# Cross attention with a routed expert layer: six of eight score units as 16-bit pairs, and a new order of norm, dispatch, positions and first period

## What is computed

```python
xn = layernorm(x)
q = xn @ Wq.T + bq;  k = ctx @ Wk.T + bk;  v = ctx @ Wv.T + bv      # 16 heads of 16, 77 context rows
scores = q . k / 4, masked;  attn = softmax(scores)
x = x + (attn . v) @ Wo.T + bo
xf = layernorm(x)
probs = softmax(xf @ w_router);  gate, eidx = top_k(probs, 2);  gate /= sum(gate)
# place of a token in its expert: a running count over all tokens; capacity 768 rows of each of 8 experts
h = relu(expert_in @ w1 + b1);  y = h @ w2 + b2
x = x + sum over the two experts of gate * y
```

## Time and profile before

| | us |
|---|---|
| median of 3 runs | 554.68 (549.78 to 555.1) |
| the profiled execution, its own time | 555.85 |
| its span in the profile | 554.1 |
| TensorE busy | 474.3 (86% of the span) |
| TensorE weight loads busy | 444.1 (80%) |
| VectorE busy | 284.8 (51%) |
| ScalarE busy | 268.3 (48%) |
| GpSimd busy | 234.0 (42%) |
| mean granted TensorE clock | 0.897 |

### The profile page before, as it was taken

One profiled execution on the slowest core, in us unless ns is written; L12 is line 12 of the kernel. 1 busy time (PEld: TensorE's weight loads), 2 busy tenths in 40 slices (PEclk: granted clock), 3 DMA queues, 4 the chain that ended last, 5 costly groups with the idle time before them and its releaser, 6 DMA issues.

```text
span 554.1 us, 10225 instructions
## 1 busy us (share of the span) xinstructions
PE 474.3 (86%) x3757; PEld 444.1 (80%) x3757; DVE 284.8 (51%) x579; ACT 268.3 (48%) x507; POOL 234.0 (42%) x364
## 2 busy tenths in 40 slices
PE   5474989999898978515999999999999999999990
PEld 4353878787777857415999999999999999999990
DVE  3447274788775633211564563745537455465430
ACT  2225254466363541202866765567755577654520
POOL 4612021434744337473043643636436365363531
PEclk9879598999996865655999999999999999999995
DMA  8838289843273101213033341433414334131110
GB/s 259 199 109 265 78 229 279 218 115 123 88 210 115 49 30 48 68 67 117 1 122 101 129 133 39 159 116 141 130 29 165 114 113 147 27 97 38 48 38 1
DMA packets 51767, 63.07 MB, mean 114 GB/s; under 512 B 7515, under 2 KB 46474, under 8 KB 51598
## 3 DMA queue, kind: packets, MB, share of 16 engines
q1 hardware_dynamic: 36118, 41.10, 25.5%
q0 software_dynamic: 6144, 12.64, 6.9%
q10 hardware_dynamic: 9464, 8.79, 5.8%
HBM read 40.97 MB, written 25.72 MB: 120 GB/s over the span
## 4 chain that ended last, share of the span: by engine, by line
PE 59%; POOL 7%; issue 4%; DVE 3%; ACT 1%; DMA 1%; POOLq 0%; DVEq 0%; SPq 0%
PE ps L1161 16%; PE ps L1159 16%; PE ps L1160 16%; POOL expert_in L526 3%; PE ps L1441 2%; PE ps L1260 2%; PE ps L1285 1%; PE ps L1174 1%; PE ps L1304 1%; ACT rows L687 1%; POOL rstd L420 1%; POOL rows L515 1%; DMA xc<-expert_in 1%; DMA expert_in<-rows,sidx 0%; PE ps L1242 0%
## 5 line engine op out<-in xcount | busy, mean ns | idle before, releaser
L792 ACT ACTIVATE hf<-ps,bcol 128x256 f32<-128x256 f32 x192 | 80.0, 468 | 97.1 <-PE ps L1161 97.0
L1159 PE MATMUL ps<-wh,hh 128*128 128x256 f32 x384 | 109.5, 285 | 0.0
L1159 PE MATMUL ps<-xTh,wh 128*128 128x256 f32 x384 | 108.7, 283 | 0.0
L1161 PE MATMUL ps<-xTh,wl 128*128 128x256 f32 x384 | 108.6, 283 | 0.0
L1160 PE MATMUL ps<-xTl,wh 128*128 128x256 f32 x384 | 108.5, 282 | 0.0
L1161 PE MATMUL ps<-wh,hl 128*128 128x256 f32 x384 | 107.7, 280 | 0.0
L1160 PE MATMUL ps<-wl,hh 128*128 128x256 f32 x384 | 107.7, 280 | 0.0
L1110 DVE TENSOR_TENSOR hl<-hf,hh 128x512 fp32r<-128x512 f32 x96 | 66.6, 694 | 78.1 <-ACT hh L798 73.8
L575 POOL DMA_INDIRECT out<-yb,ctok x48 | 51.9, 1082 | 92.8 <-DVE yb L1125 84.3
L567 POOL DMA_INDIRECT acc<-out,ctok x48 | 69.3, 1444 | 37.4 <-issue 22.9
L1159 PEld LDWEIGHTS ps<-xTh,wh 128*128 128x128 f32 x384 | 73.9, 193 | 0.0
(11 more groups left out here) (163 smaller groups left out, 854.7 us busy)
## 6 DMA issues: line engine op xcount, KB each, us to landing
wraw<-in_L_ffn_w SPq DMA_DIRECT2D x16, 1024.0 KB
expert_in<-zrow ACTq DMA_DIRECT2D x6, 1032.0 KB, 7.6
xc<-expert_in SPq DMA_DIRECT2D x24, 258.0 KB
qs<-q_by_head SPq DMA_DIRECT2D x8, 768.0 KB, 5.9
q_by_head<-qh SPq DMA_DIRECT2D x16, 256.0 KB, 2.7
q_by_head<-ql SPq DMA_DIRECT2D x8, 256.0 KB, 3.8
out<-xs SPq DMA_DIRECT2D x4, 512.0 KB
xs<-in_x ACTq DMA_DIRECT2D x1, 1536.0 KB, 11.7
```

The lines of the kernel that those rows point to most:

```text
L792: ins = a.activation(hf[:, i % 2, s * CH:(s + 1) * CH], ps[:, i, s * CH:(s + 1) * CH], ACT.Relu, bias=bcol[:, bass.ds(at(e * MT + 2 * i + ...
L1159: T.matmul(dst, sh, mh, start=first, stop=False)
L1161: return T.matmul(dst, sl, mh, start=False, stop=last)
```

## The change

It has four parts.

1. Of a period's eight units six are split (0, 1, 2, 4, 5, 6) and two plain (3, 7); before it was four and four. `rest_p(i, j)` runs for j = 0 to 5.
2. On POOL a period now reads `tag_rows(n-1)` (the two copies of token number and gate, taken out of `dispatch`), `norm2(n)`, `picks(n-1)`, `dispatch(n-1)`, `norm1(i+3)`, `running(n)`.
3. `positions(n-1)` stands behind `times_v(w,0)` on TensorE, `slot_values(n-1)` and `picked(n-1)` in the first half of VectorE's period. `scores(m,0)` waits for one slot value more from m = 4 on.
4. In the head, q(0) is turned and projected ahead of k. V's projection, Wo's turn, the front of macro tile 2 and the copies and rests of v are in period 0.

VectorE's order within a period is written anew with this; in it `rest_q(f)` comes ahead of `maximum(i+1,0)`, where it came behind it.

```diff
-    NS = NG // 2
+    SPLIT = (0, 1, 2, 4, 5, 6)
+    PLAIN = (3, 7)
+    NS, NF = len(SPLIT), len(PLAIN)
...
@@ POOL
+            def tag_rows(n):
+
+                pool.wait_ge(S["gates_ready"], n + 1)
+                if n >= 2:
+                    pool.wait_ge(S["scattered%d" % (n % 2)], n // 2 * (2 * G * 16))
+                g.tensor_copy(rows[:, n % 2, :, :, TOK], tokid[:, toks(n), :])
+                g.tensor_copy(rows[:, n % 2, :, :, GATE], gt[:, n % 2])
...
+                if n >= 1:
+                    tag_rows(n - 1)
                 if n >= 0:
                     norm2(n)
-                if i + 3 < NM:
-                    norm1(i + 3)
-                if n >= 0 and i < NM:
-                    running(n)
                 if n >= 1:
                     picks(n - 1)
...
                 if n >= 1:
                     dispatch(n - 1)
-                if n >= 0 and i >= NM:
+                if i + 3 < NM:
+                    norm1(i + 3)
+                if n >= 0:
                     running(n)
...
@@ VectorE, the period
-                units, nxt, front, tail, slots = i < NM, i + 1 < NM, 3 <= f < NM, 0 <= w < NM, n >= 0
+                units, nxt, front, tail, slots = i < NM, i + 1 < NM, f < NM, 0 <= w < NM, n >= 0
...
                 if units:
                     rest_p(i, 0)
+                if i == 0:
+                    values()
                 if tail:
                     sum_o(w, 0)
-                if nxt:
-                    maximum(i + 1, 0)
+                if n >= 1:
+                    slot_values(n - 1)
+                if units:
+                    rest_p(i, 1)
                 if front:
                     rest_q(f)
                 if nxt:
-                    maximum(i + 1, 1)
+                    maximum(i + 1, 0)
                 if tail:
                     divide_o(w, 0)
+                if n >= 1:
+                    picked(n - 1)
+                if nxt:
+                    maximum(i + 1, 1)
                 if units:
-                    rest_p(i, 1)
+                    rest_p(i, 2)
                 if i == 0:
-                    v_rest(1)
-                if slots and i >= NM:
-                    picked(n - 1)
+                    v_rest(0)
                 if nxt:
                     maximum(i + 1, 2)
                 if tail:
                     sum_o(w, 1)
+                if units:
+                    rest_p(i, 3)
                 if nxt:
                     maximum(i + 1, 3)
                     split_max(i + 1)
                 if tail:
                     divide_o(w, 1)
-                if units:
-                    rest_p(i, 2)
+                if i == 0:
+                    v_rest(1)
                 if i + 3 < NM:
                     stats1(i + 3)
                 if units:
-                    rest_p(i, 3)
+                    rest_p(i, 4)
+                    rest_p(i, 5)
                 if i == 0:
                     rest_bo()
...
@@ TensorE
-                    if m >= 5:
-                        pe.wait_ge(S["slot_ready"], m - 4)
+                        pe.wait_ge(S["slot_ready"], m - 3)
...
+            turn_xn(0)
+            pe.wait_ge(S["wq_copied"], 1)
+            project_q(0)
             pe.wait_ge(S["wk_copied"], 1)
...
                 if tail:
                     times_v(w, 0)
+                if n >= 1:
+                    positions(n - 1)
```

More of the change, by code:

```diff
@@ L178, in xattn_moe_kernel @@
         pf = at_("pf", [KV, 2, 2 * GT])
[L179 removed]
+        pn = at_("pn", [KV, 2, NF, 2 * GT])
         st = at_("st", [P, G, 6])
@@ L984, in v_rest, with values @@
                 ins.then_inc(S["vpart_step"], 1)
+            def values():
+                dve.wait_ge(S["v_projected"], 1)
+                dve.wait_ge(S["bv_loaded"], 16)
+                dve.wait_ge(S["const_ready"], 3)
+                for b in range(NB):
+                    ins = v.scalar_tensor_tensor(out=vf[:, b * D:(b + 1) * D], in0=bv_b[:], scalar=bscale[0:KV],
+                                                 in1=ps[0:KV, 4, b * D:(b + 1) * D], op0=ALU.mult, op1=ALU.add)
+                ins.then_inc(S["vf_ready"], 1)
             stats1(0)
@@ L989, in _ @@
             normal1(0)
+            stats1(1)
+            dve.wait_ge(S["mask_loaded"], 16)
+            v.tensor_scalar(mb[:, :, 0:NK], mraw[:], 0.0, NEG, ALU.is_equal, ALU.mult).then_inc(S["mask_step"], 1)
+            rest_q(0)
+            normal1(1)
             dve.wait_ge(S["k_projected"], 1)
@@ L1014, in _ @@
             maximum(0, 1, ST)
-            dve.wait_ge(S["v_projected"], 1)
-            dve.wait_ge(S["bv_loaded"], 16)
-            dve.wait_ge(S["const_ready"], 3)
-            for b in range(NB):
-                ins = v.scalar_tensor_tensor(out=vf[:, b * D:(b + 1) * D], in0=bv_b[:], scalar=bscale[0:KV],
-                                             in1=ps[0:KV, 4, b * D:(b + 1) * D], op0=ALU.mult, op1=ALU.add)
-            ins.then_inc(S["vf_ready"], 1)
             maximum(0, 2, SC)
@@ L1090, in _ @@
                     route(n)
-                    if n >= 1 and i < NM:
-                        slot_values(n - 1)
-                if slots:
-                    if n >= 1 and i < NM:
-                        picked(n - 1)
                     gates(n)
@@ L1341, in _ @@
             ins.then_inc(S["k_projected"], 1)
-            turn_xn(0)
-            pe.wait_ge(S["wq_copied"], 1)
-            project_q(0)
             pe.wait_ge(S["wv_loaded"], 16)
@@ L1353, in _ @@
             project_q(1)
-            turn_xn(2)
             pe.wait_ge(S["kst_loaded"], 16 * 4)
             pe.wait_ge(S["mask_copied"], 1)
-            scores(0, 0, SC, 2)
-            scores(0, 1, ST, 2)
-            pe.wait_ge(S["bias_copied"], 1)
-            pe.wait_ge(S["wv_copied"], 1)
-            for b in range(NB):
-                for k in range(KT):
-                    ins = T.matmul(ps[0:KV, 4, b * D:(b + 1) * D], cT[:, k, b, :], wvT[:, k, :],
-                                   start=(k == 0), stop=(k == KT - 1))
-            ins.then_inc(S["v_projected"], 1)
-            scores(0, 2, SC, 2)
-            scores(0, 3, ST, 2)
-            pe.wait_ge(S["wo_loaded"], 16)
-            turn_weight(3, 5, "wo_turned")
+            for p in range(PAIRS):
+                scores(0, p, (SC, ST)[p % 2], 2)
             turn_max(0)
-            project_q(2)
             pe.wait_ge(S["sel_ready"], 4)
@@ L1377, in _ @@
                 f, w, n = i + 2, i - 1, i - 2
-                units, nxt, front, tail, slots = i < NM, i + 1 < NM, 3 <= f < NM, 0 <= w < NM, n >= 0
+                units, nxt, front, tail, slots = i < NM, i + 1 < NM, f < NM, 0 <= w < NM, n >= 0
                 if units:
                     scores_t(i, 0)
+                if i == 0:
+                    pe.wait_ge(S["wv_copied"], 1)
+                    for b in range(NB):
+                        for k in range(KT):
+                            ins = T.matmul(ps[0:KV, 4, b * D:(b + 1) * D], cT[:, k, b, :], wvT[:, k, :],
+                                           start=(k == 0), stop=(k == KT - 1))
+                    ins.then_inc(S["v_projected"], 1)
+                    pe.wait_ge(S["wo_loaded"], 16)
+                    turn_weight(3, 5, "wo_turned")
                 if front:
@@ L1424, in _ @@
                 if slots:
-                    if n >= 1 and i < NM:
-                        positions(n - 1)
                     logits(n)
@@ L1431, in _ @@
                     project_o(w)
-                if slots and i >= NM - 1:
-                    positions(n)
+            positions(NM - 1)
             def turn_x(c, par, half):
```

75 lines of the change are left out of this document (31 added, 44 removed).

## The result

| | before | changed kernel |
|---|---|---|
| median | 554.89 us (549.78 to 555.15, 4 runs) | 580.07 us (577.87 to 581.5, 4 runs) |
| ratio, 95% interval | | 1.0473 (1.0404 to 1.0542) |
| span of the profiled execution | 554.1 us | 579.8 us |
| mean granted clock of TensorE | 0.897 | 0.843 |

The changed kernel is 4.7% slower; the forecast was 582 us.

What follows compares the result with a forecast made beforehand. TensorE's program order was taken to bound periods 3 and 4. On the 554.1 us span, -3 +11 +16.6 +1 +12.5 -11 +1 gave 582 us; likeliest range 572 to 598, 560 to 600 with (a).

Steps and rivals of the forecast that it cites:

- Head, -3: Before period 0: k readied behind q, V's work moved out; period 0 starts near 38.3 us in place of 41.2.
- Period 0, +11: Period 0, 16 to about 27 us: moved work, `rest_q` idle and two `rest_p` stand ahead of VectorE's bias chain.
- `rest_q` ahead of the first maximum: Periods 0 to 5: TensorE idles 3.4 us more each, awaiting the maximum; +16.6 us over periods 1 to 5.
- The clock, 2.5 for each of five periods: Periods 1 to 5: each idle lowers TensorE's clock, costing nothing to 4.9 us; taken as 2.5, together +12.5.
- (c): Even, 549 to 560 us: period 0 grows only 6.5, periods 6, 7 and tail gain 15.4; chance 0.07.
- (d): Rival: TensorE's weight loads set the time, waits on maxima are off the path; faster, 531 us; chance 0.06.
- (a): Rival: the same waits, but the clock stays up through the idles; about 570 us (560 to 572); chance 0.20.
- (b): Rival: all periods cold, the clock not recovering before the next idle; 606 us; chance 0.07 for over 600.
- Six split units: Every period: two more split units save TensorE 0.7 us a tile, 1.4 us a period, 11 us over eight.
- Period 6, +1: Period 6, which has no `rest_q`: 1 us longer.
- Period 7 and the tail, -11 and +1: Period 7 and tail: second norm ahead of dispatch removes stall and clock fall, -11; POOL late in last part, +1.
- What would show it: Signs of being right, among them scores waiting 3.5 to 3.9 us, period 3 over 23 us, `turn_o` waiting for `o`.

Runs made afterwards that it cites:

- e1: Changed kernel with the first maximum moved back ahead of `rest_q` on VectorE: 552.22 us, ratio 0.997.
- 2: Kernel before with one exchange alone, `rest_q` put ahead of the first maximum on VectorE: 589.66 us, ratio 1.064.
- e3: Changed kernel with 28 unused matmuls in TensorE's idle ahead of the second group of scores, periods 0 to 5: 565.99 us, ratio 1.022.
- e5: Kernel before with six split units and two plain ones alone; head, POOL's order and first maximum's place unchanged: ratio 1.007.
- e8: e1 with the bias chain at the head's end and macro tile 3's statistics at period 0's start: 549.62 us, ratio 0.984.
- e10: Kernel before with POOL's new order, positions, slot values and picks early, maximum first, bias chain and macro tile 3's statistics early: 540.04 us, ratio 0.977.
- e9: e5 with 13 unused matmuls a period ahead of the third and fourth scores and `turn_o`: 558.96 us, ratio 1.006.
- 4: Changed kernel with VectorE's bias chain moved from the end of period 0 to the head, ahead of `maximum(0,0)`: 579.37 us, ratio 1.046.
- e11: e10 with the same unused matmuls as e9: 543.29 us, ratio 0.980.

## Why the prediction was right, and where it was not

The total was 2 us off, and the sign and its cause were right. Part of the closeness is luck: the terms were off by -0.8 (head), +1.5 (period 0), -1.6 (periods 1 to 5), -2.9 (period 6) and +1.4 (period 7 and tail), 2.4 us less in all. The terms, one by one (periods by the table, other parts by the experiments):

- **Head, -3.** -3.8 in the profiled execution; the means of the old head in eight traces and the new one in five, 40.3 and 37.5, give -2.8. Period 0 started at 37.45 (38.3 foretold), the first scores at 30.0 (31.1).
- **Period 0, +11.** +12.5. The wait for the bias is 6.7 us, as named. Some 3 of it are `rest_q` (28.5 against 25.5 in e1), the other 9.5 the moved work in front of the chain.
- **`rest_q` ahead of the first maximum.** The wait itself: 3.4 us more idle foretold, 3.1 more measured (3.52 in place of 0.44), and `nm` ends 2.35 us behind the second exp, exactly as laid out (113.12 less 110.77); the 0.3 too much came in by setting TensorE's start at 113.5 behind a maximum that ends at 113.12. Experiments 1 and 2 show that this step alone makes the loss. Its delay was foretold to pass through to the period's end in full; experiment 3 shows about 14 us in the whole kernel, 12 of them in periods 1 to 5 (122.4 against 110.5), 2.4 of the 3.1 us each time. The term of 16.6 us for these five periods still fits, since with the maximum first they are already 4.1 us longer than before (110.5 against 106.4), and 12 and 4.1 make 16. Some of the delay went into small waits that were there anyway: the list of waits of the kernel before has

```profile
PE ps L1216 <- DVE nm L869: 8.7, 14, 2.3
```

  where the changed one has 7 waits with 21.4 us: not about 20 us more, as foretold, but 12.7, since the many short waits had gone.
- **The clock, 2.5 for each of five periods.** 2.3 in the mean by experiment 3, so the sum was right in size. But it was right as a mean only: the filler gave back 3.9, 4.2 and 3.6 us in periods 1 to 3, near the row's upper bound, and nearly nothing in periods 4 and 5, where it did not keep the clock up. That upper bound was read a little low: from the second group of scores to the period's end period 3 took 12.3 us (110.10 to 122.40), so 5.2 and not 4.9. What I had not seen is the clock fall in the last stretch (57.0 us in the changed kernel, 52.4 in e1 and e3), behind idles that e1 and e3 have as well.
- **The rivals.** Neither (c) nor (d) came. (d) took the weight loads (15.95 of 19.6 us busy in period 3) for the limit; the 28 us of experiment 1 show that the wait for the maximum was on the path. (a), the same waits with the clock up, was put at 570; experiment 3, which makes just that, took 566. (b), all cold, was given 0.07; periods 0 and 1 came near it, at 0.62 and 0.64.
- **Six split units.** This step failed, though it was no term of its own in the sum: the 0.7 us a tile stands inside the layout of each period, and its 11 us in rival (d). The matmul time went as computed (1.4 us a period foretold, 1.46 measured), but by experiment 5 the kernel is 0.7% slower and periods 1 to 5 are 4 us longer. I took a period in which TensorE is busy for 18.35 of 19.6 us for one that shortens when TensorE's work does. With 1.46 us taken out, 0.8 us turned into waits for VectorE's maxima and for `o` at once, and a fall of the clock cost 1.6. I had set the busy share of weight loads against it as rival (d), not the nearness of the other chains. In the total the error was hidden: behind the new wait the changed kernel's periods were no longer bound by TensorE's own work, and the sum of +29.1 for periods 1 to 5 stands against +27.5.
- **Period 6, +1.** -1.9 in the changed kernel, though TensorE waits in it for 2.22 us for the slot values.
- **Period 7 and the tail, -11 and +1.** -8.6 in the changed kernel. The wait of 3.19 us for the second norm is gone, as foretold; x2's turn starts without idle and period 7 took 16.4 us (222.5 to 238.9) where 14.7 was laid out. What failed is that the clock fall would go with the wait: the clock fell all the same, at 233 us (windows under experiment 3), behind an idle of 0.86 us. Where it did not fall, in e1, period 7 took 14.0 us, so the layout at full clock was sound. Here too I had looked for one long idle and found none.
- **"What would show it".** The wait of 3.5 to 3.9: 3.52. Periods 3 and 4 over 23 us with a clock under 1: 27.0 and 25.1, 0.75 and 0.80. Period 0 about 27: 28.5. No idle ahead of x2's turn: right. "`turn_o` waits for `o`" was no sign at all: TensorE does so 2 times in the changed kernel, 1.3 us in all, and did so 4 times, 2.3 us in all, in the kernel before.

What stays open: why period 1 of e8 runs at 0.63 while that of e10 runs at 1.00. Both have the bias and the statistics early; they differ in the head, in V's work and in the number of split units, and no run here changes one of these alone. The trace of e8 shows only where it starts: in its period 0 TensorE waits 1.78 and 0.69 us for maxima, the clock is at 0.50 from 54 us on and comes back between 64 and 68, while in e10 it is back at 1.00 from 54 us on. Open as well is what decides whether short idles bring a fall (5 against 9, and period 7 of the changed kernel against that of e1).

## What to carry to other kernels

- On an engine that goes strictly through its own list the price of a call is not its duration but what it waits for. Before exchanging two calls of VectorE, write down for each what it waits for and who waits for it: `rest_q` takes 0.9 us and TensorE did not wait for it, but ahead of the maximum it brought two exps and `qh`, all ScalarE's, in front of TensorE, at a price of 28 to 36 us.
- If the busiest engine of a stretch is busy for nearly all of it, that alone doesn't say that less work for it makes the stretch shorter. Look how close the next chain is; here 0.8 of the 1.46 us saved turned into waits at once. The windows show the first, only the list of small waits the second.
- When a removed wait gives nothing, look for the next wait a few microseconds later and for the clock behind it (4). A move that gave nothing by itself can still be worth keeping as one of two (8, 10).
- A filler belongs in the idle, so it must stand ahead of the wait that ends last, and it must not be larger than the idle. In 9 it stood behind that wait and took more than the change had saved.

## What the runs showed of the hardware

- The granted clock of TensorE falls not only behind one long idle. In e5 it fell behind four idles of 0.24 to 0.87 us between 108 and 117 us, in the changed kernel's period 7 behind three of 0.71, 0.27 and 0.86. The Trainium skill ("TensorE: Matmul & The Clock Gate", "Why this matters for your kernels") names in its list only a long idle between bursts; by that line alone none of these falls would have come.
- The same idles don't always bring a fall. With the same three in period 7, at the same places, the clock stayed at 1.00 in e1 and e3 for about another 9 us. And in e9 an idle of 1.87 us and 3.2 us of idle in period 3 brought none. From the idles alone no run here lets one tell.
- Unused matmuls in an idle of 3.5 us raised the mean clock of the kernel (0.889 against 0.843) and saved 14 us, though TensorE executed 168 matmuls more; 4.6 of the 14 lie where there is no filler. In e9 the clock stayed at 1.00 in periods 2 to 4 and in e11 in periods 2 to 5, but the filler saved nothing.
